# GpSimd takes two more of the eight state reads in the last three bodies of a merged recurrence loop

## The reference

```python
def step(s, rkvw):
    r_t, k_t, v_t, w_t = rkvw
    a = k_t[..., :, None] * v_t[..., None, :]
    out = jnp.einsum('bhi,bhij->bhj', r_t, u * a + s)
    s = a + w_t[..., :, None] * s
    return (s, out)
...
og = ((og - m) / jnp.sqrt(va + 1e-05)).reshape(b, l, e) * gn_w + gn_b
x1 = x + og * g @ Wo.T
xc = _ln(x1, ln2_w, ln2_b)
...
rr = jax.nn.sigmoid(xr2 @ Wfr.T)
kk = jnp.square(jax.nn.relu(xk2 @ Wfk.T))
return x1 + rr * (kk @ Wfv.T)
```

## Time and profile before

| what | value |
|---|---|
| three runs | 1209.41, 1212.56 and 1212.60 us (median 1212.56) |
| the profiled execution | 1213.37 us, of which 1211.6 us are the span in the profile |
| TensorE clock granted over the span | 0.982 of full speed |
| busy over the span | PE 94%, DVE 80%, ACT 64%, POOL 49% |
| the three early bodies | about 1006 to 1131 us from the span's start |
| body 14, from DVE's first multiply to that of body 15 | 1049.36 to 1092.98 us |

### The profile page before, as it was taken

How to read it: one execution, slowest core, us unless ns; L and a number is a source line. 1 busy time by engine, 2 the same in 40 slices (tenths; PEclk the granted TensorE clock), 3 DMA queues, 4 the chain that set the end, 5 groups by cost and what they waited for, 6 DMA issues and landing times.

```text
span 1211.6 us, 35521 instructions
## 1 busy us (share of the span) xinstructions
PE 1136.8 (94%) x13568; PEld 963.8 (80%) x13568; DVE 969.1 (80%) x1677; ACT 777.1 (64%) x1752; POOL 593.9 (49%) x520
## 2 busy tenths in 40 slices
PE   5899999999999998999999999999999998987788
PEld 5889888888998877887788878888788876765667
DVE  5987778787777742288999999999999999999654
ACT  4778777777787754655665556655566546654464
POOL 4787787877877830333434333343434434233111
PEclk9999999999999989999999999999999999998899
DMA  9400000111111100000000000000000000000001
GB/s 334 130 4 1 0 1 3 29 38 47 40 39 43 35 2 1 1 1 1 2 1 1 1 1 1 0 0 0 0 0 0 0 2 1 18 9 9 18 28 60
DMA packets 25535, 27.31 MB, mean 23 GB/s; under 512 B 2336, under 2 KB 20064, under 8 KB 25056
## 3 DMA queue, kind: packets, MB, share of 16 engines
q1 hardware_dynamic: 25440, 25.99, 6.5%
HBM read 21.79 MB, written 4.19 MB: 21 GB/s over the span
## 4 chain that ended last, share of the span: by engine, by line
PE 69%; DVE 14%; issue 13%; POOL 2%; ACT 1%; DMA 0%; DVEq 0%; ACTq 0%; POOLq 0%
PE psum L945 9%; PE psum L353 9%; PE psum L954 7%; PE psum L267 5%; PE psum L1034 4%; PE psum L336 4%; PE psum L368 4%; PE psum L1071 3%; PE psum L297 3%; PE psum L280 3%; DVE shared L1723 3%; PE psum L1115 2%; PE psum L310 2%; DVE shared L1717 2%; PE psum L994 2%
## 5 line engine op out<-in xcount | busy, mean ns | idle before, releaser
L1723 DVE TENSOR_TENSOR_SCAN shared<-late_wT,shared 128x512 f32<-128x512 f32 x128 | 184.5, 1442 | 4.4
L856 POOL TENSOR_TENSOR late_xm<-late_mixed,late_xa 128x512 f32<-128x512 f32 x80 | 96.0, 1208 | 162.3 <-DVE late_mixed L1691 156.0
L232 POOL TENSOR_TENSOR shared<-shared,att_row_max 128x512 f32<-128x512 f32 x128 | 132.5, 1055 | 17.8 <-DVE att_row_max L564 17.8
L353 PE MATMUL psum<-shared 128*128 128x128 f32 x1024 | 127.3, 279 | 1.0 <-ACT shared L462 1.0
L453 ACT ACTIVATE shared<-shared 128x512 f32<-128x512 f32 x128 | 80.4, 631 | 69.7 <-POOL shared L232 69.6
L954 PE MATMUL psum<-w,late_hT 128*128 128x256 f32 x512 | 122.1, 383 | 1.0 <-ACT late_hT L1335 0.9
L353 PEld LDWEIGHTS psum<-shared 128*128 128x128 f32 x1024 | 121.4, 195 | 1.4 <-ACT shared L462 1.4
L865 POOL TENSOR_TENSOR shared<-shared,late_rT 128x512 f32<-128x512 f32 x32 | 40.7, 1273 | 164.0 <-DVE shared L1723 164.0
L945 PE MATMUL psum<-late_glnT,w 128*128 128x256 f32 x512 | 118.4, 385 | 1.8 <-ACT late_glnT L1326 1.8
L1717 DVE TENSOR_TENSOR shared<-psum,shared 128x504 f32<-128x504 f32 x128 | 86.7, 677 | 40.9 <-PE psum L1071 39.5
L564 DVE TENSOR_REDUCE att_row_max<-shared 128x8 f32<-128x512 f32 x128 | 86.7, 679 | 40.5 <-POOL shared L225 40.5
(11 more groups left out here) (160 smaller groups left out, 2672.0 us busy)
## 6 DMA issues: line engine op xcount, KB each, us to landing
shared<-in_enc SPq DMA_DIRECT2D x64, 128.0 KB, 2.6
out<-x SPq DMA_DIRECT2D x16, 256.0 KB, 2.0
x<-in_x SPq DMA_DIRECT2D x7, 512.0 KB, 9.5
w<-in_w SPq DMA_DIRECT2D x2, 1024.0 KB, 17.6
shared<-in_cross_mask SPq DMA_DIRECT2D x1, 1024.0 KB, 12.4
shared<-in_w_qkv SPq DMA_DIRECT2D x1, 768.0 KB, 4.7
x<-in_x SPq DMA_DIRECT2D x2, 256.0 KB, 3.9
shared<-in_w_kv SPq DMA_DIRECT2D x1, 512.0 KB, 13.2
```

The lines of the kernel that those rows point to most:

```text
L232: nc.gpsimd.tensor_tensor(zs, zs, peak.unsqueeze(2).to_broadcast([P, PAIRS, S]), ALU.subtract).then_inc(shifted, 1)
L353: last = nc.tensor.matmul(dst[:, half * P:(half + 1) * P], w[:, kb, c0 + half * P:c0 + (half + 1) * P], src[:, u % 2, kb, 0:P], start=(kb ...
L856: nc.gpsimd.tensor_tensor(xm[:, m % 2, :, :].rearrange("p h (b t) -> p (h b) t", t=S), mixed[:, m % 2, :, :].rearrange("p h (b t) -> p (h ...
L1723: nc.vector.tensor_tensor_scan(states, wT[:, u, half, :, :, :].rearrange("p j b t -> p (j b t)"), states, 0.0, ALU.mult, ALU.add).then_inc ...
```

## The change

In the bodies 13, 14 and 15 GpSimd makes the reads of q = 3 as well, groups 6 and 7, and DVE no longer makes them. The two new reads stand in GpSimd's list behind the `mix` step of the same `n`: read 6 between `mix` steps 3 and 4, read 7 between `mix` step 4 and `scale`. The counts that `sum_heads` waits for are worked out anew (`reads_by`). In the other thirteen bodies nothing changes.

```diff
+        def on_gpsimd(r, q):
+            return q == POOL_SUM or q == SUMS - 1 and early(r)
+
+        def reads_by(r, q, gpsimd):
+            first = r if not early(r) else RUNS - 3
+            done = first * PER_SUM * (1 if gpsimd else SUMS - 1)
+            if early(r):
+                done += (r - first) * PER_SUM * 2
+            return done + PER_SUM * sum(on_gpsimd(r, i) == gpsimd for i in range(q + 1))
...
-                    if n * JG // JQ == POOL_SUM and there(s):
+                    if n // PER_SUM == POOL_SUM and there(s):
                         read(s, u, n)
                     if n >= 3 and there(s + 1):
                         mix(s + 1, n - 3)
+                    if n // PER_SUM != POOL_SUM and there(s) and on_gpsimd(s, n // PER_SUM):
+                        read(s, u, n)
...
-                if q == POOL_SUM:
-                    pe.wait_ge(pool_read_ready, (r + 1) * PER_SUM)
+                if on_gpsimd(r, q):
+                    pe.wait_ge(pool_read_ready, reads_by(r, q, True))
                 else:
-                    pe.wait_ge(read_ready, r * (GROUPS_R - PER_SUM) + (q + 1 - int(q > POOL_SUM)) * PER_SUM)
+                    pe.wait_ge(read_ready, reads_by(r, q, False))
...
             def read(r, u, n):
-                if n // PER_SUM == POOL_SUM:
+                if on_gpsimd(r, n // PER_SUM):
                     return
```

## The result

The changed kernel takes 1220.11 us (median of seven runs, 1214.78 to 1220.64). The kernel before took 1212.24 us in the same comparison (1209.41 to 1212.79, seven runs). The ratio is 1.0061, with a 95% interval of 1.0044 to 1.0078, so it is slower by 5 to 10 us. The forecast was 1217.0 us and slower; its direction was right and its size low. The stated range ended at 1220.0: the median is 0.1 us above that, and the ratio on the 1212.56 us from which the forecast started gives 1219.96, just inside.

A forecast was written before the change was run, and what follows sets the result against it. PE was taken to be bound by waiting for POOL's `scale` at the ends of bodies 13 and 14. Delays of 2.19 and 2.18 us, with 0 for the clock, added 4.4 to 1212.56, giving 1217.0 us; range 1213.2 to 1220.0.

The forecast's parts named there:

- `scale` is what PE waits for, and the reads make it late: Ends of bodies 13 and 14: reads queued ahead delay `scale`, and PE takes each delay in full, 4.4 us.
- The size of it: `scale` was to end 2.19 us late in body 13 and 2.18 us late in body 14.
- The rule that instructions with all operands in SBUF take turns between DVE and GpSimd: Scans, reads and `scale` go one after another; behind the other engine a scan needs 1.09 us more, `scale` 0.89.
- without it `scale` would have been 0.64 us late: Body 13 bound with no sharing between DVE and POOL: `scale` 0.64 us late, 1.3 us for both places.
- Body 15 hides its reads: End of body 15: both reads are hidden beside other work; nothing lost, nothing won.
- The cover: End of body 15: slack left of 1.7 us before PE asks for `scale` and 0.9 us at DVE's step awaiting ACT.
- I take 0: Behind PE's longer waits for `scale`, TensorE's lower clock was to last no longer than before: 0 us added.
- The stated bounds: Extra cost of TensorE's clock staying low behind both longer waits for `scale`: 0 to 2.6 us.
- The rival named for it: Lower clock lasts longer behind PE's longer waits: 1.3 to 2.6 us on top, 1218.3 to 1219.6; chance 0.17.
- What the profile was to show: PE's waits for `scale` about 3.2 and 4.6 us, DVE busy down 5 to 6 us, POOL up 7.6.
- One sign: DVE's waits for `ch_values` in bodies 14 and 15 grow from 0.29 and 1.92 us by over 2 us each.

The follow-up runs named there:

- e1: Changed kernel with GpSimd's reads of groups 6 and 7 moved behind `scale`: 1210.49 us, ratio 0.9991 to the kernel before.
- e5: Changed kernel with only read 7 moved behind `scale`, read 6 staying ahead of the last `mix` step: 1211.06 us, ratio 0.9995 to the kernel before.
- the two filled kernels: Changed kernel and kernel before, each with unused PE products at the waits for `scale` and ahead of `mix_pair`: 1211.53 and 1207.30 us.
- e3: Kernel before with the change made in body 15 alone: 1211.61 us, ratio 0.9989.
- e2: Kernel before with the change made in body 13 alone: 1217.14 us, ratio 1.0039.
- e6: Kernel before with unused PE products at the waits for `scale`, two in body 14 and four in body 15: 1210.87 us, ratio 1.0003.
- e11: Kernel before with unused PE products at the waits for `scale` (two, four) and six ahead of `mix_pair` in bodies 13 and 14: 1207.30 us, ratio 0.9948.
- e12: Kernel before filled at the waits for `scale`, ahead of `mix_pair`, and at three places in body 15 (five, four, eight products): 1207.41 us, ratio 0.9978.

## Why the prediction was right, and where it fell short

- **`scale` is what PE waits for, and the reads make it late.** Right, and shown: moved behind `scale`, the same reads cost nothing that could be told (`e1`), and read 7 alone is to blame (`e5`).
- **The size of it.** 2.19 and 2.18 us were worked out; the ledger has 2.14 and 2.15, and the two filled kernels are 4.30 us apart in their traces for 4.4 forecast. `mix` step 4 ended at 1046.59 (46.65 forecast), read 7 ran 1047.75 to 49.01 (47.83 to 49.10), `scale` ended at 1050.98 (51.08). The rule that instructions with all operands in SBUF take turns between DVE and GpSimd carried the sum step by step: without it `scale` would have been 0.64 us late. The Trainium skill's page SBUF — State Buffer ("SBUF: two separate sides") states it for VectorE instructions with two inputs in SBUF, and says that the one that comes second blocks fully. The order of the rows agrees: the 2.18 us scan ends 1.07 us behind GpSimd's step. But 1.07 us is less than the 1.22 that a scan takes alone, and the 0.88 us that `scale` needs behind a scan less than its 1.31, so a part of the second instruction's length isn't held up.
- **Body 15 hides its reads.** Right (`e3`). The cover was thinner than said: `transpose_on` came at 1139.40, 1.15 us behind the end of `scale`, not 1.7, and DVE's step behind the four mixing steps waited 0.60 us more for ACT, not 0.9.
- **"I take 0" for the clock.** This is the term that was mis-sized. It was argued from two waits, 1.06 and 2.37 us, behind which the clock was down for the same 3.4 us. At 3.19 and 4.52 us it was down for about twice that, and a new stretch came at 1066, behind a wait that hadn't grown (2.76 us). It measured 3.2 us in the ledger and 3.8 between the kernels. The stated bounds were 0 to 2.6 us, so they missed it too. The rival named for it ("the clock stays down longer", 0.17) is what happened, on top of the forecast. The length of the wait doesn't settle it: in the trace of `e2` the clock behind the same 3.19 us was down no longer than before. Such stretches come and go from one execution to the next, and taking one trace for the price was the weak step. That the range held, by 0.04 us on the ratio, is luck.
- **What the profile was to show.** The waits came out as forecast (3.2 and 4.6 us said, 3.19 and 4.52 found), and the chain that ended last passes through the reads and `scale` at both places, `scale` with 2.02 us. GpSimd's busy time rose by 5.5 us (599.4 for 593.9), not 7.6, as its other instructions ran less hindered: `make_bonus` took 1.28 us for 1.74, the last `scale` of the bodies 1.09 for 1.98. DVE's fell by 6.2. One sign was wrong: DVE's waits for `ch_values` grew by 1.1 and 0.9 us only (1.36 and 2.85), not by over 2, because DVE had lost the rest ahead of it, waiting 3.14 us for ACT's copy, which itself hangs on `transpose_on`. The delay was passed on whole; it stood in other rows than I had said.

What stays open: which of PE's pauses brings a lower stretch of the clock. Pauses of 1.06, 1.93, 2.37 and 2.76 us each had one in some executions, and the one of 1.93 and that of 2.76 us had none in others. In `e6` a stretch turned up at the next pause when the waits for `scale` were filled, and `e11` filled that pause too; this is read from one trace of each.

## What to carry to other kernels

Ask of an engine with idle time what stands at the end of its queue. GpSimd was idle half of the span and was still what PE waited for at these two places. A read of 1.26 us put directly ahead of that last step made it 2.1 us late, since the read has to wait for its own input there; the same read behind the step cost nothing that could be told, and that is a matter of one line. And where TensorE waits anyhow, don't price the lengthening of a wait at its length alone: here the clock took almost as much again (3.8 us for 4.2). It does so in some executions and not in others, so a single trace doesn't give its price. Compare the granted clock of all runs as well.

## What the runs showed of the hardware that I had not expected

- The granted clock fell in pieces: 3.4 us at half level behind waits of 1.06 and 2.37 us, about 6.8 us behind 3.19 and 4.52 us, and once at an unchanged wait of 2.76 us. In the changed kernel it cost 3.2 us of 7.2. The 3.19 us wait of `e2` had 3.4 us behind it, so the length of the wait alone doesn't decide.
- Products of no use made a kernel faster: six ahead of `mix_pair` and two or four at the waits for `scale` took the kernel before from 1212.76 to 1207.30 us (0.9948).
- A clock kept up in one place can be lost in another: in `e12` the products at 1125 took 1.99 us in place of 3.40 in `e11`, which won 1.4 us there, and products in the tail took 3.48 in place of 1.96. The kernel took the 1207.4 us of `e11` (1207.3).
